# The order of one attention step in a decoder-layer kernel: values ahead of scores, head transposes apart, side products on other places

## What is computed

```python
x = x + attn(layernorm(x))           # rmsnorm, 16 heads of 64, softmax(q k / 8) v, out projection
x = x + cross(context, layernorm(x)) # one head of 128 over 512 context rows
x = x + ffn(layernorm(x))            # 128 -> 512 -> 128, both products on quantised values

def attn(h):
    q, k, v = (einsum('bsd,dhe->bshe', h, w) for w in (wq, wk, wv))
    w = softmax(einsum('bqhd,bkhd->bhqk', q * 64 ** -0.5, k))
    return einsum('bqhe,hed->bqd', einsum('bhqk,bkhd->bqhd', w, v), w_out) + b_out
```

## Time and profile before

| | |
|---|---|
| median of 3 runs | 396.38 us (396.37 to 396.95) |
| profiled execution | 396.12 us, of which the span of instructions 394.2 us |
| PE busy | 379.1 us, 96% of the span |
| DVE busy | 323.8 us, 82% |
| ACT busy | 259.0 us, 66% |
| POOL busy | 164.1 us, 42% |
| one middle batch | 43.60 to 43.86 us |

### The profile page before, as it was taken

The page is one execution under the profiler, slowest core; times in us unless marked ns, Lnnn a source line. Parts: engine busy times, 40 slices in busy tenths (PEclk is TensorE's granted clock), DMA queues, the critical chain, the costliest instruction groups (busy, mean ns, idle before and its releaser), DMA issues.

```text
span 394.2 us, 9104 instructions
## 1 busy us (share of the span) xinstructions
PE 379.1 (96%) x3012; PEld 286.3 (73%) x3012; DVE 323.8 (82%) x776; ACT 259.0 (66%) x805; POOL 164.1 (42%) x179
## 2 busy tenths in 40 slices
PE   8999999999999999999999999999999999998975
PEld 7778777777777777777777767777778777776422
DVE  4988779869897789869896889869895998766994
ACT  4976676666668566766677656767676768725674
POOL 3665444534544345525554345434454344511000
PEclk9999999999999999999999999999999999999999
DMA  7500000001000100001000100001000000000003
GB/s 233 153 17 2 2 2 0 3 2 40 2 3 2 40 0 0 0 0 40 0 0 0 40 0 0 0 0 40 0 0 0 27 2 2 2 2 0 0 2 106
DMA packets 12310, 7.50 MB, mean 19 GB/s; under 512 B 1280, under 2 KB 11264, under 8 KB 12288
## 3 DMA queue, kind: packets, MB, share of 16 engines
q1 hardware_dynamic: 11856, 6.69, 5.7%
q10 hardware_dynamic: 432, 0.52, 0.4%
HBM read 6.16 MB, written 1.05 MB: 18 GB/s over the span
## 4 chain that ended last, share of the span: by engine, by line
PE 66%; DVE 19%; issue 9%; ACT 2%; DVEq 1%; DMA 1%; POOL 1%; POOLq 0%; ACTq 0%
PE turned_bank L474 13%; PE o_bank L483 12%; PE score L464 12%; PE acc_bank L490 5%; DVE negmax L925 3%; DVE pT L932 3%; PE side_bank L447 3%; PE q_bank L447 3%; PE q_bank L448 3%; PE q_bank L449 3%; PE side_bank L541 3%; DVE h_max L1248 2%; PE side_bank L448 2%; PE side_bank L449 2%; PE side_bank L537 2%
## 5 line engine op out<-in xcount | busy, mean ns | idle before, releaser
L1292 POOL TENSOR_TENSOR prob<-prob,rinv 128x512 f32<-128x512 f32 x128 | 132.8, 1045 | 146.4 <-DVE rinv L929 146.4
L749 ACT ACTIVATE prob<-score,negmax 128x256 f32<-128x256 f32 x252 | 117.6, 475 | 71.7 <-DVE negmax L925 70.0
L925 DVE TENSOR_REDUCE negmax<-score 128x2 f32<-128x512 f32 x126 | 85.9, 682 | 26.8 <-PE score L464 25.4
L932 DVE COPY pT<-turned_bank 128x512 f32<-128x512 f32 x124 | 84.2, 679 | 7.0 <-PE turned_bank L474 6.6
L474 PE MATMUL turned_bank<-ident,prob 128*128 128x128 f32 x496 | 81.0, 286 | 1.7 <-DVE pT L932 1.2
L474 PEld LDWEIGHTS turned_bank<-ident,prob 128*128 128x128 f32 x496 | 52.0, 141 | 33.6 <-issue 24.2
L483 PE MATMUL o_bank<-pT,v_sb 128*64 128x256 f32 x512 | 69.4, 392 | 0.6 <-ACT oT L740 0.6
L749 ACT ACTIVATION_READ_ACCUMULATOR prob<-score,negmax 128x1 f32 x252 | 51.2, 203 | 0.0
L483 PEld LDWEIGHTS o_bank<-pT,v_sb 128*64 128x64 f32 x512 | 31.1, 136 | 19.9 <-issue 8.2
L740 ACT ACTIVATE q_hi<-q_bank 128x512 fp32r<-128x512 f32 x63 | 38.2, 606 | 10.6 <-PE q_bank L449 9.7
L917 DVE TENSOR_TENSOR q_lo<-q_bank,q_hi 128x512 fp32r<-128x512 f32 x63 | 42.8, 680 | 0.0
(11 more groups left out here) (230 smaller groups left out, 618.7 us busy)
## 6 DMA issues: line engine op xcount, KB each, us to landing
c_sb<-in_ctx_dram SPq DMA_DIRECT2D x8, 256.0 KB, 3.0
x_sb<-in_x_dram SPq DMA_DIRECT2D x8, 128.0 KB, 2.8
out_dram<-xn_all SPq DMA_DIRECT2D x4, 256.0 KB, 2.9
big<-in_L_attn_wk_dram ACTq DMA_DIRECT2D x2, 256.0 KB, 4.7
big<-in_L_attn_wq_dram SPq DMA_DIRECT2D x2, 256.0 KB, 5.7
big<-in_L_attn_wv_dram SPq DMA_DIRECT2D x2, 256.0 KB, 6.3
wo_sb<-in_L_attn_w_out_dram SPq DMA_DIRECT2D x1, 512.0 KB, 7.7
w_sb<-in_L_ffn_w_dram SPq DMA_DIRECT2D x2, 256.0 KB, 4.7
```

Of the source, the lines that this page charges most:

```text
L749: last = nc.scalar.activation(prob[:, slot, t, :], banks[r][:, t * S:(t + 1) * S], ACT.Exp, bias=negmax[:, slot, t:t + 1], scale=1.0, accu ...
L925: nc.vector.tensor_reduce(negmax[:, slot], banks[r][:].rearrange("p (t k) -> p t k", k=S), X_AXIS, ALU.max, negate=True).then_inc(max_done, 1)
L932: nc.vector.tensor_copy(pT[:, slot].rearrange("p k q -> p (k q)"), bank[:]).then_inc(pT_done, 1)
L1292: nc.gpsimd.tensor_tensor(prob[:, slot], prob[:, slot], rinv[:, slot].unsqueeze(2).to_broadcast([P, QT, S]), ALU.mult).then_inc(prob_done, 1)
```

## The change

It alters the order in the steps of all engines, and no operation.

- TensorE's step is now: wait for `o_done`, `project_out`, `project_qk`, side product 0, head 0 turned, `values`, `scores`, side product 1, head 1 turned. The very first step ("opening") keeps the scores ahead of the turned heads.
- Side products: TC and W2 of step 0 change places, W3 moves from step 2 to step 1 (second place), PX0 from step 4 to 5, PX1 from 5 to 6, UX to the second place of step 6, OX and V0 to step 7.
- ScalarE's step: side 0, `split_hi`, copy of the values, side 1, both exponentials.
- VectorE's step: norm work, side 0, copy of head 0, statistics, maxima of head 0, aggregate, maxima of head 1, side 1, copy of head 1, residual, `split_lo`, `normalise` of the second norm, both reciprocals at the end. The residual moves from step 1 to the end of step 0.
- GpSimd's inverse roots follow the norms to their new steps.

```diff
--- before.py
+++ after.py
@@ -50,8 +50,8 @@
 
 
 
-PLACE = {(0, 0): "W2", (0, 1): "TC", (1, 0): "W1", (2, 0): "W3", (2, 1): "TX", (3, 0): "QX", (3, 1): "TH",
-         (4, 0): "SX0", (4, 1): "PX0", (5, 0): "SX1", (5, 1): "PX1", (6, 0): "UX", (6, 1): "OX", (7, 0): "V0"}
+PLACE = {(0, 0): "TC", (0, 1): "W2", (1, 0): "W1", (1, 1): "W3", (2, 1): "TX", (3, 0): "QX", (3, 1): "TH",
+         (4, 0): "SX0", (5, 0): "SX1", (5, 1): "PX0", (6, 0): "PX1", (6, 1): "UX", (7, 0): "OX", (7, 1): "V0"}
 PAIRS_PER_BATCH = 8
 PREPARE = ["TH", "V0"]
 OWN = ["W1", "W2", "W3"]
@@ -64,6 +64,8 @@
 PLACES = {"first": {k: t for k, t in PLACE.items() if t in [*PREPARE, *OWN]}, "mid": PLACE, "last": LAST_PLACE}
 
 PLACES["first"] |= {(3, 0): "XW", (5, 0): "XE"}
+PLACES["first"][0, 0] = PLACES["first"].pop((0, 1))
 TASKS = {kind: [places[k] for k in sorted(places)] for kind, places in PLACES.items()}
 TASKS["start"] = [*PREPARE]
 PAIRED = ["TC", "TH", "TX", "QX", "XW"]
@@ -549,22 +551,32 @@
 
             def step(kind, b, parity, i, j):
                 g = b * PAIRS + j
-                more_q, more_scores, cross = ahead(kind, j, 3), ahead(kind, j, 2), kind != "first"
+                more_q, more_scores = ahead(kind, j, 3), ahead(kind, j, 2)
                 if kind == "first" and j == 1:
                     pe.wait_ge(wqk_lo_done, 4)
+                opening = kind == "first" and j == 0
+                if not opening:
+                    wait(pe, o_done, g - 1)
+                if not (kind == "first" and j < 2):
+                    if j == 2:
+                        wait(pe, x1_done, b)
+                    if kind == "first" and j == 2:
+                        pe.wait_ge(load_wo, 16)
+                    project_out((j - 2) % PAIRS)
                 if more_q:
                     project_qk((j + 3) % PAIRS, parity if j < PAIRS - 3 else 1 - parity, q_banks[(j + 3) % 2])
                 if task := side_at(kind, j, 0):
                     side(kind, b, 1 - parity, i, task)
-                if cross and j == 1:
-                    pe.wait_ge(o_done, g - 1)
-                    project_out(PAIRS - 1)
-                if more_scores:
+                def scores_ahead():
                     pe.wait_ge(q_lo_done, g + 3)
 
-                    pe.wait_ge(exp_done, 2 if kind == "first" and j == 0 else 2 * g + 4)
+                    pe.wait_ge(exp_done, 2 if opening else 2 * g + 4)
                     scores(j % 2)
+                if opening:
+                    scores_ahead()
                 pe.wait_ge(prob_done, 2 * g + 1)
                 wait(pe, pT_done, copied_before(kind, g, j, 0))
                 turn_probs(2 * j % 8, turned_in(kind, j, 0))
@@ -573,24 +585,19 @@
                     pe.wait_ge(prob_done, 2 * g + 2)
                     pe.wait_ge(pT_done, copied_before(kind, g, j, 1))
                     turn_probs(2 * j % 8 + 1, turned_in(kind, j, 1))
-                if not (kind == "first" and j < 1):
-                    wait(pe, o_done, g - 1)
-                if j != 1 and not (kind == "first" and j < 2):
-                    if j == 2:
-                        wait(pe, x1_done, b)
-                    if kind == "first" and j == 2:
-                        pe.wait_ge(load_wo, 16)
-                    project_out((j - 2) % PAIRS)
-                if task := side_at(kind, j, 1):
-                    side(kind, b, 1 - parity, i, task)
-                if not (kind == "first" and j < 1):
+                if not opening:
                     if j == 1:
-                        pe.wait_ge(side_free, side_index(kind, b, "W1"))
+                        pe.wait_ge(side_free, side_index(kind, b, "W2") + 1)
+                    if j == 5:
+                        pe.wait_ge(side_free, side_index(kind, b, "W3") + 1)
                     if late(kind, j):
                         pe.wait_ge(pT_done, 2 * g)
                     slot = 2 * (j - 1) % 4
                     values((j - 1) % PAIRS, (slot, slot + 1), 1 - parity if j == 0 else parity)
+                if more_scores and not opening:
+                    scores_ahead()
+                if task := side_at(kind, j, 1):
+                    side(kind, b, 1 - parity, i, task)
                 if not no_scores:
                     pe.wait_ge(prob_done, 2 * g + 2)
                     pe.wait_ge(pT_done, copied_before(kind, g, j, 1))
@@ -786,22 +793,24 @@
             def step(kind, b, parity, i, j):
                 g = b * PAIRS + j
                 more_scores = ahead(kind, j, 2)
+                opening = kind == "first" and j == 0
+                if (task := side_at(kind, j, 0)) and not opening:
+                    side(kind, b, 1 - parity, task)
                 if ahead(kind, j, 3):
                     act.wait_ge(q_raw, g + 4)
                     split_hi((j + 3) % 2, q_banks[(j + 3) % 2])
-                if task := side_at(kind, j, 0):
+                if opening:
+                    side(kind, b, 1 - parity, task)
+                else:
+                    act.wait_ge(o_raw, g)
+                    copy(oT[:, (j - 1) % 2], o_bank[:, 0:S]).then_inc(o_done, 1)
+                if task := side_at(kind, j, 1):
                     side(kind, b, 1 - parity, task)
                 if more_scores:
                     act.wait_ge(max_done, 2 * g + 5)
                     exps(0, (2 * j + 4) % 8)
-                if task := side_at(kind, j, 1):
-                    side(kind, b, 1 - parity, task)
-                if more_scores:
                     act.wait_ge(max_done, 2 * g + 6)
                     exps(1, (2 * j + 5) % 8)
-                if not (kind == "first" and j < 1):
-                    act.wait_ge(o_raw, g)
-                    copy(oT[:, (j - 1) % 2], o_bank[:, 0:S]).then_inc(o_done, 1)
                 if kind == "last" and j == 1:
                     act.wait_ge(w_inv_done, 1)
                     for c in range(FT):
@@ -1053,63 +1062,63 @@
                 g = b * PAIRS + j
                 prepare, cross = kind != "last", kind != "first"
                 more_scores = ahead(kind, j, 2)
-                if ahead(kind, j, 1) and not (kind == "first" and j == 0):
-                    dve.wait_ge(exp_done, 2 * g + 4)
-                    invert_sums((2 * j + 3) % 8)
-                if kind == "mid" and j == PAIRS - 1:
-                    aggregate(2, b, *PLAIN_NORM)
-                if kind == "mid" and j == 0:
-                    dve.wait_ge(load_x[1 - parity], (i + 2) * 16)
-                    statistics(0, tiles(x_sb[:, 1 - parity]), b + 2)
-                if cross and j == 2:
-                    normalise(1, tiles(xn2), tiles(x1_sb), b, xn2_done)
+                opening = kind == "first" and j == 0
+                if cross and j == 1:
+                    aggregate(1, b, *PLAIN_NORM)
                 if prepare and j == 3:
                     normalise(0, tiles(xn1), tiles(x_sb[:, 1 - parity]), b + 2, xn1_done)
                 if task := side_at(kind, j, 0):
                     side(kind, b, 1 - parity, task)
-                if cross and j == 1:
-                    residual(b, 1 - parity)
-                if more_scores:
+                if kind == "mid" and j == PAIRS - 1:
+                    dve.wait_ge(side_free, side_index(kind, b, "OX") + 1)
+                if opening:
                     dve.wait_ge(score_raw, 2 * g + 5)
                     maxima(0, (2 * j + 4) % 8)
                 dve.wait_ge(pT_raw, 2 * g + 1)
                 keep_turned(2 * j % 4, turned_in(kind, j, 0))
-                if kind == "first" and j == 0:
+                if opening:
 
                     dve.wait_ge(exp_done, 4)
                     invert_sums(3)
-                no_scores = kind == "last" and j >= PAIRS - 2
-                if no_scores:
-                    dve.wait_ge(pT_raw, 2 * g + 2)
-                    keep_turned(2 * j % 4 + 1, turned_in(kind, j, 1))
+                if prepare and j == 1:
+                    if kind == "first":
+                        dve.wait_ge(load_x[1], 16)
+                    else:
+                        dve.wait_ge(load_x[1 - parity], (i + 2) * 16)
+                    statistics(0, tiles(x_sb[:, 1 - parity]), b + 2)
+                if kind == "mid" and j == PAIRS - 1:
+                    statistics(2, x2_of(b), b)
+                if more_scores and not opening:
+                    dve.wait_ge(score_raw, 2 * g + 5)
+                    maxima(0, (2 * j + 4) % 8)
+                if prepare and j == 1:
+                    aggregate(0, b + 2, *FIRST_NORM)
+                if kind == "mid" and j == PAIRS - 1:
+                    aggregate(2, b, *PLAIN_NORM)
                 if more_scores:
                     dve.wait_ge(score_raw, 2 * g + 6)
                     maxima(1, (2 * j + 5) % 8)
-                if kind == "first" and j == 0:
-                    dve.wait_ge(load_x[1], 16)
-                    statistics(0, tiles(x_sb[:, 1]), 2)
-                if prepare and j == 0:
```

(29 more changed lines are left out.)

## The result

The changed kernel takes 396.00 us (median of 12) against 397.01 us for the kernel before, timed beside it: ratio 0.9979, 95% interval 0.9970 to 0.9988. It is faster by 0.2%, about 1 us, where the prediction said 3.7 us. The profiled execution took 395.93 us, its span is 394.1 us (before 394.2). In the file after, lines lie 2 to 9 further: transposes L476, values L485, scores L466, maxima L934, copy to pT L941, exponentials L756.

What follows compares the result with a forecast made beforehand. TensorE was taken to bound the kernel. Handover -12.2, middle-batch stalls +7.5 and ends +1.0 summed to -3.7 us, from 396.4 to 392.7 us; range 385 to 400.

Steps and rivals of the forecast that it cites:

- Bound: Whole loop: TensorE-bound in six of eight batches, small waits for others; middle batches 43.4 us after, instead of 43.7.
- The saving of the handover: TensorE, values straight to scores: one shape switch fewer, 0.20 us at each of 61 places, 12.2 us saved.
- Stalls of middle batches: TensorE waiting for late VectorE work in steps 0 to 4: 2.25 us per batch against 1.0 before, +7.5 us over six.
- The ends: First and last batch: stalls add 0.5 us each, +1.0 us together.
- half of these extras are missing: First and last batch: only half the middle batches' extra VectorE work in steps occurs, hence +0.5 us each.
- Rival 3: Steps 1 and 3: head 1's copy late, VectorE operations held by paired GpSimd scales; 398.1, to 401 us; chance 0.19.
- Rival 1: VectorE keeps up: slack in steps 5 to 7 absorbs extras, stalls stay 1.0; 384.2, up to 387 us; chance 0.24.
- Rival 2: Values to scores: handover costs 0.40 us, so no TensorE time is saved; 398.9 us; chance 0.10.
- Rival 4: Between values and scores: scores wait for q's lower halves, so the two don't join; 396 to 400 us; chance 0.05.
- Waits on TensorE's queue, ScalarE, GpSimd, DMA: 0: Reordered waits and copies on these queues add nothing in the loop, apart from 0.1 us allowed in step 4.
- ScalarE's 0: ScalarE's value copy and second side product ahead of the exponentials cost 0, since score banks are free in time.

Runs made afterwards that it cites:

- v1: Changed kernel with aggregate, normalisation, cross normalisation ahead of the reciprocals (steps 0, 2, 7), head 1's copy ahead of second maxima in light steps: 386.70 us, ratio 0.9751.
- k1: Changed kernel with VectorE's copy of head 1 ahead of the second maxima in steps without a second side product: 395.44 us, ratio 0.9968.
- a1: Changed kernel with the second norm's aggregate moved from the start of step 1 to step 0's end, ahead of the reciprocals: 392.56 us, ratio 0.9894.
- n1: Changed kernel with the normalisation of x moved from step 3 to step 2, ahead of the reciprocals, in the first batch alone: 395.20 us, ratio 0.9962.
- u1: Changed kernel with TensorE's scores put back ahead of head 0's transposes in every step, undoing the handover: 423.51 us, ratio 1.0675.
- s2: v1 plus a one-column full-shape matmul between values and scores at each of 61 handovers: 392.85 us against 386.70 timed beside it.

## Why the prediction failed

It forecast -2.1 us for the middle batches and -1.6 for the two ends. The middle gave -2.5 and the ends +2.1. By its own steps:

- **Bound** (TensorE, small waits): right. Middle batches were said to be 43.4 us and are 43.2 (259.25 / 6). That they came so near is partly luck, see the next two points.
- **The saving of the handover, 0.20 us per place: too large.** Steps with the same side products compare directly. Without any, 4.26 us before and 4.10 with the copy ahead: 0.16. With UX and OX 6.43 and 6.33: 0.10. About 0.98 per middle batch is an estimate from these (six steps at 0.11, two at 0.16), not 1.6. v1, whose middle batches have next to no waits, gives 0.75 (42.74, the prediction's own count without stalls, less 41.99). Per place that is 0.09 to 0.12, and 61 places give 5.7 to 7.5 us, not 12.2.

Where the rest goes, the weight loads of a step without side products show: the kernel before, then k1.

```profile
41.91 0.19 PEld L447 LDWEIGHTS q_bank<-ht_hi,wqk_hi 128*128 128x128 f32 x1
...
42.83 0.19 PEld L464 LDWEIGHTS score<-q_hi 64*128 64x128 f32 x2
...
44.12 0.53 PEld L490 LDWEIGHTS acc_bank<-wo_sb,oT 128*128 128x128 f32 x4
44.77 0.63 PEld L483 LDWEIGHTS o_bank<-pT,v_sb 128*64 128x64 f32 x8
```

```profile
48.46 0.19 PEld L449 LDWEIGHTS q_bank<-ht_hi,wqk_hi 128*128 128x128 f32 x1
...
49.19 0.46 PEld L476 LDWEIGHTS turned_bank<-ident,prob 128*128 128x128 f32 x4
49.82 0.63 PEld L485 LDWEIGHTS o_bank<-pT,v_sb 128*64 128x64 f32 x8 [0.17 <-issue]
```

Before, the scores follow the projection after 0.92 us, 0.21 over its stream of 0.71: the price that the prediction read, and it is gone. But the new neighbours cost more than the old. The transposes follow the projection after 0.73 (0.02 over), and the values follow the transposes after 0.63, 0.24 over their 0.39, where they followed the output projection after 0.65, 0.21 over its 0.44. That leaves 0.16. In the step of UX another 0.04 goes at UX and the transposes behind it (2.16 us for both in the trace after, 88.38 to 90.54; apart 1.73 and 0.39). The prediction counted the places where the shape changes and gave each one price, whatever stood ahead of it.

- **Stalls of middle batches, 2.25 us: too many, in the right places.** 43.21 less the 41.76 to 41.99 of a batch without stalls is 1.2 to 1.45. Against v1, step 0 has 0.43 (said 0.2), step 1 0.63 (said 1.05), step 3 0.15 (said 0.65), step 2 none (said 0.25). The mechanism of the largest, veps held by a scale until 1.9 us into the step, was the one that a1 took away. Two errors of 0.6 to 1.0 us per batch, the saving too large and the stalls too many, cancelled: the good total was luck in its size, not in its mechanism.
- **The ends, +0.5 each for stalls: this is the step that failed most.** Forecast -0.9 for the first batch (7 x 0.20 less 0.5), measured +1.75; forecast -0.7 for the last (6 x 0.20 less 0.5), measured +0.32. The text reasoned "half of these extras are missing". It had the loop in hand ("frees TensorE at 4.2, against 3.7 + side products") and priced it nowhere, although a step without side products is 0.5 us short, and such steps are most of the first batch. k1 gave 1.03 of it back in the trace. A further 1.0 is XW behind a held normalisation (n1): XW occurs in the first batch only and was not looked at. The smaller saving of the handover is at least 0.5 (7 x 0.08). Together that is some 2.5 of the 2.65 us.
- In the last batch 1.0 us are to be told: 0.5 is the smaller saving (6 x 0.08), 0.3 PX0 and PX1. **The other 0.2 stays open**; early scores are not it.
- **Rivals.** Rival 3's mechanism (tensor-scalar operations held by paired scales) was real, but all the stalls of a middle batch, 1.2 to 1.45 us, stay far below the 2.9 from which it decides. Rival 1 (VectorE keeps up) is v1's case: 386.7 where it said 384.2 to 387, though v1 gets there with a smaller saving and with the stalls of the kernel before gone too. Rival 2 (a handover that saves nothing) was too dark, but the measured 0.09 to 0.16 lie between it and the forecast. Rival 4 did not occur.
- "Waits on TensorE's queue, ScalarE, GpSimd, DMA: 0" held in the loop. u1 shows that ScalarE's 0 hung on the handover: its copy ahead of the exponentials is free only while values come ahead of scores.

## What to carry to other kernels

A loop of engines has a shortest turn: here from scores by way of maxima, copy, transposes and values to the next scores. Count it once for the step with the least other work, and price it at the ends of the program, where such steps are: there a gain of the long steps turns into a loss. Here small vector operations did better ahead of the operation that releases a GpSimd pass than behind it; moving such operations and one copy brought 9.3 us, on top of a new order that alone had brought 1.0. What a removed change of tile shape saves is read from what stands next to what afterwards, not from a count of changes. And when a change orders several engines anew, undoing it on one of them measures nothing of its worth.

## What the hardware did that was not expected

A one-column full-shape matmul between two tiled groups costs 0.10 us per place (s2), load to load 0.11, with no sign of the 0.2 us that stands behind longer streams. A GpSimd scale that starts 0.16 us before a 0.17 us VectorE operation of 128x2 (147.90 and 148.06) holds it for 0.73 us more, until that scale of 1.04 us ends.
